# Conditional transformer block, eight groups in staggered beats: first norm begun four beats ahead of its old place, opening reordered, clears of va on VectorE, oT copied ahead of tanh

## Reference

```python
def _tc_rmsnorm(x, t, gw, gb, bw, bb):
    g = (t @ gw.T + gb)[:, None, :]
    b = (t @ bw.T + bb)[:, None, :]
    inv_rms = jax.lax.rsqrt(jnp.mean(x * x, axis=-1, keepdims=True) + EPS)
    return g * x * inv_rms + b

# attention: 16 heads of 8 features, softmax(q k^T / sqrt(8)) v, then Wo
# swiglu:    silu(x @ gate_w.T) * (x @ hid_w.T) @ out_w.T, 512 hidden features
y = x + _attention(_tc_rmsnorm(x, t, g1w, g1b, b1w, b1b), Wq, Wk, Wv, Wo)
y = y + _swiglu(_tc_rmsnorm(y, t, g2w, g2b, b2w, b2b), gate_w, hid_w, out_w)
out = x + y
```

## Time and profile before

| | us |
|---|---|
| median of 3 runs | 274.45 (273.54 to 274.57) |
| profiled execution | 273.25 |
| its span, first to last instruction | 271.2 |
| TensorE matmul busy | 228.1 (84%) |
| VectorE busy | 204.4 (75%) |
| ScalarE busy | 164.2 (61%) |
| GpSimd busy | 111.9 (41%) |

### The profile page before, as it was taken

How to read it: one execution, slowest core, us unless ns; L and a number is a source line. 1 busy time by engine, 2 the same in 40 slices (tenths; PEclk the granted TensorE clock), 3 DMA queues, 4 the chain that set the end, 5 groups by cost and what they waited for, 6 DMA issues and landing times.

```text
span 271.2 us, 8235 instructions
## 1 busy us (share of the span) xinstructions
PE 228.1 (84%) x3048; PEld 179.9 (66%) x3048; DVE 204.4 (75%) x489; ACT 164.2 (61%) x353; POOL 111.9 (41%) x183
## 2 busy tenths in 40 slices
PE   2436558977898999999999999999999899899895
PEld 2314236644666877787788778876887678677794
DVE  4655663497789798879887988888887888445573
ACT  5436373677586767775777677567656565565330
POOL 8244732173826272627262736252623232323320
PEclk9999755599999999999999999999999999999999
DMA  6758400260044004400350035003500000000001
GB/s 186 294 152 197 123 2 10 59 175 4 6 110 127 3 27 114 130 15 24 96 141 24 24 81 157 23 25 79 158 22 24 4 22 2 24 2 21 23 19 39
DMA packets 18818, 18.77 MB, mean 69 GB/s; under 512 B 3644, under 2 KB 17980, under 8 KB 18652
## 3 DMA queue, kind: packets, MB, share of 16 engines
q1 hardware_dynamic: 18252, 17.80, 23.4%
q10 hardware_dynamic: 528, 0.46, 0.7%
HBM read 3.22 MB, written 2.10 MB: 20 GB/s over the span
## 4 chain that ended last, share of the span: by engine, by line
PE 40%; issue 29%; POOL 14%; DVE 11%; ACT 5%; POOLq 0%; ACTq 0%
PE pv L423 5%; PE proj L483 5%; PE ffn L317 4%; PE score L406 3%; DVE nmax L748 3%; PE ffn L319 3%; PE ffn L318 3%; PE tok L442 2%; POOL inv L910 2%; POOL xn_lo L923 2%; PE raw L379 2%; PE proj L345 2%; POOL inv L881 2%; PE tok L438 2%; POOL xs L916 2%
## 5 line engine op out<-in xcount | busy, mean ns | idle before, releaser
L748 DVE TENSOR_REDUCE nmax<-raw 128x8 f32<-128x1024 f32 x61 | 74.2, 1217 | 6.7 <-PE raw L379 6.6
L591 ACT ACTIVATE p_s<-score 128x1024 f32<-128x1024 f32 x64 | 65.5, 1023 | 15.7 <-PE score L406 14.5
L423 PE MATMUL pv<-p_s,va 128*32 128x128 f32 x1024 | 42.8, 287 | 0.9 <-ACT xn L609 0.4
L620 ACT ACTIVATE th<-ffn 128x256 f32<-128x256 f32 x53 | 20.3, 384 | 27.7 <-PE ffn L319 27.4
L317 PE MATMUL ffn<-xn_hi,ffn_hi 128*128 128x256 f32 x106 | 34.7, 327 | 0.0
L483 PE MATMUL proj<-ffn_out_s,hT 128*128 128x128 f32 x256 | 33.8, 275 | 0.3 <-DVE x_s L816 0.3
L805 DVE SCALAR_TENSOR_TENSOR gated<-th,ffn 128x256 f32<-128x256 f32 x53 | 22.0, 415 | 15.8 <-ACT th L620 15.5
L483 PEld LDWEIGHTS proj<-ffn_out_s,hT 128*128 128x128 f32 x256 | 31.2, 191 | 0.6 <-issue 0.5
L423 PEld LDWEIGHTS pv<-p_s,va 128*32 128x32 f32 x1024 | 25.2, 112 | 8.5 <-issue 3.2
L319 PE MATMUL ffn<-xn_hi,ffn_lo 128*128 128x256 f32 x106 | 29.7, 280 | 0.0
L318 PE MATMUL ffn<-xn_lo,ffn_hi 128*128 128x256 f32 x106 | 29.6, 279 | 0.0
(11 more groups left out here) (123 smaller groups left out, 469.1 us busy)
## 6 DMA issues: line engine op xcount, KB each, us to landing
ks<-kp SPq DMA_DIRECT2D x48, 128.0 KB, 2.4
qs<-qp SPq DMA_DIRECT2D x45, 128.0 KB, 2.5
out_y<-x_s SPq DMA_DIRECT2D x16, 128.0 KB, 1.8
x_s<-in_x SPq DMA_DIRECT2D x1, 1536.0 KB, 9.6
qs<-shift SPq DMA_DIRECT2D x64, 4.0 KB
x_s<-in_x SPq DMA_DIRECT2D x2, 256.0 KB, 3.5
ffn_in_s<-in_ffn_in_w SPq DMA_DIRECT2D x1, 512.0 KB, 6.2
qs<-qp ACTq DMA_DIRECT2D x3, 128.0 KB, 3.6
```

Of the source, the lines that this page charges most:

```text
L423: mm = pe.matmul(pv[VW * j:VW * j + VW, (t % 2) * L:(t % 2 + 1) * L], va[vbuf(g)][:, t // 2, at:at + VW], p_s[:, (BEATS * g + t) % PBUF, p ...
L591: act.activation(p_s[:, n % PBUF, :], score[:], ACT.Exp, scale=SCALE).then_inc(s_exp, 1)
L748: dve.tensor_reduce(heads[:, :, t % 2, :], raw_dst(g, t)[:].rearrange("l (e j m) -> l e j m", e=HALVES, j=HQ), AX.X, ALU.max, negate=True) ...
```

## The change

MEAN moves from -24 to -28: squares, inverse root and scaling of a group are due four beats earlier, at T = 4, 12, 20 and 28 for groups 4 to 7; those of group 3, formerly in beat 0, go into the opening. In ScalarE's beat, the squares move from ahead of tanh to behind it, and the oT copy from behind tanh to ahead of it. In the opening, TensorE does the transposes of group 2 behind the fifth raw product and the transpose of maxima, alternating two banks; the two clears of va go from ScalarE to VectorE; VectorE does the high and low part of group 0 and the high parts of group 1 in another order; GpSimd sets the ones of the first va buffer ahead of the inverse root of group 2.

```diff
--- before.py
+++ after.py
@@ -61,7 +61,7 @@
     SCALE = float(DH) ** -0.5
     assert D == 128 and L == 128 and W == 512 and B % (2 * NB) == 0 and H * DH == D and HC == 4
 
-    MEAN, XT1, HI1 = -24, -23, -15
+    MEAN, XT1, HI1 = -28, -23, -15
     VALUE, KEY, QUERY = -7, -14, -13
     STACK = -12
     RAW, MAXT = -7, -3
@@ -219,7 +219,7 @@
         def xt1_dst(g, b):
             if g < 2:
                 return (score[:, 0:L], score[:, 512:512 + L], raw[:, 0:L], raw[:, 512:512 + L])[b]
-            return tok[:, 0:L] if early(g) else score[:, (b % 2) * 512:(b % 2) * 512 + L]
+            return (tok, ffn)[b % 2][:, 0:L] if early(g) else score[:, (b % 2) * 512:(b % 2) * 512 + L]
 
         def raw_dst(g, t):
             return score if g == 0 and t % 2 and t < BEATS - 1 else raw
@@ -326,7 +326,8 @@
                 elif g == 1:
                     pe.wait_ge(s_xn1, b + 1)
                 elif early(g):
-                    pe.wait_ge(s_xn1, NB * g + b)
+                    pe.wait_ge(s_xn1, NB * g + max(b - 1, 0))
+                    pe.wait_ge(s_qrest, 2)
                 pe.transpose(xt1_dst(g, b), xs1[:, g % 2, b, :], ident[:]).then_inc(s_xt1, 1)
 
             def a_values(g):
@@ -503,11 +504,11 @@
             b_raw(0, 1)
             a_values(0)
             b_raw(0, 2)
-            a_transpose(2, 0)
             b_raw(0, 3)
-            a_transpose(2, 1)
             b_raw(0, 4)
             b_maxT(0, 0)
+            a_transpose(2, 0)
+            a_transpose(2, 1)
             b_raw(0, 5)
             a_transpose(2, 2)
             b_raw(0, 6)
@@ -660,13 +661,10 @@
             a_middle(1, s_krest, k_rest, kp, s_kmid)
             a_middle(1, s_qrest, q_rest, qp, s_qmid)
             a_mean(2)
-            zero_fill(va[0][:].rearrange("l b v -> l (b v)"), s_va0[0])
-            a_norm(2, 0)
-            a_norm(2, 1)
             a_values(0)
-            a_norm(2, 2)
-            a_norm(2, 3)
-            zero_fill(va[1][:].rearrange("l b v -> l (b v)"), s_va0[1])
+            a_mean(3)
+            for b in range(NB):
+                a_norm(2, b)
             for T in range(LAST + 1):
                 for g, _ in due(T, KEY + 1, since=2):
                     a_high(g, s_k, key_dst(g), kp, s_khi)
@@ -678,12 +676,12 @@
                     c_ot(g, i)
                 for g, _ in due(T, KEY + 1, since=2):
                     a_middle(g, s_krest, k_rest, kp, s_kmid)
-                for g, _ in due(T, MEAN, since=3):
-                    a_mean(g)
+                for g, i in due(T, TRO, NB, 2):
+                    c_oT(g, i)
                 for g, p in due(T, FFN, PIECES):
                     d_tanh(g, p)
-                for g, i in due(T, TRO, NB, 2):
-                    c_oT(g, i)
+                for g, _ in due(T, MEAN, since=4):
+                    a_mean(g)
                 for g, i in due(T, XT2, NB, 2):
                     d_norm(g, i)
                 for g, b in due(T, XT1, NB, 2, since=3):
@@ -821,6 +819,10 @@
 
                 dve.memset(qs[u][:].bitcast(F32), 0.0).then_inc(s_zeroq[u], 1)
 
+            def zero_values(u):
+
+                dve.memset(va[u][:], 0.0).then_inc(s_va0[u], 1)
+
             dve.memset(ones[:], 1.0).then_inc(s_ones, 1)
             zero_queries(0)
             a_mean(0)
@@ -828,15 +830,18 @@
             a_mean(1)
             dve.wait_ge(s_attnw, 16)
             dve.tensor_copy(qk_hi[:], attn_w_s[:, 0:2, :]).then_inc(s_whi, 1)
+            a_hi(0, 0)
+            lo_first(0)
             scale_first(1)
-            for n in range(2):
-                a_hi(0, n)
-                lo_first(n)
+            a_hi(0, 1)
+            lo_first(1)
+            zero_values(0)
             a_rest(0, key_dst(0), kp, k_rest, s_khi, s_klo, s_krest)
-            a_rest(0, query_dst(0), qp, q_rest, s_qhi, s_qlo, s_qrest)
             a_hi(1, 0)
             a_hi(1, 1)
+            a_rest(0, query_dst(0), qp, q_rest, s_qhi, s_qlo, s_qrest)
             lowest_first(q_rest, qp, s_qmid, s_qlo)
+            zero_values(1)
             a_rest(1, key_dst(1), kp, k_rest, s_khi, s_klo, s_krest)
             a_rest(1, query_dst(1), qp, q_rest, s_qhi, s_qlo, s_qrest)
             for t in range(HQ):
@@ -965,9 +970,11 @@
             a_lo(1, 1)
             a_lowest(1, k_rest, kp, s_kmid, s_klo)
             a_lowest(1, q_rest, qp, s_qmid, s_qlo)
+            surround_values(0)
             a_inv(2)
             a_scale(2)
-            surround_values(0)
+            a_inv(3)
+            a_scale(3)
             zero_queries(2)
             zero_keys(2)
             surround_values(1)
```

## The result

The changed kernel takes 260.11 us (median of 4, 259.37 to 261.01) against 274.0 (273.07 to 274.57): ratio 0.950, 95% interval 0.9455 to 0.954.

A forecast was written before the change was run, and what follows sets the result against it. TensorE was taken as the bound from beat 8 on, with waits and a lower clock before. 12.8 us gained less 4.7 lost gave 8.1, so 266.3 us against the median of 274.45; range 261.5 to 271.0.

The forecast's parts named there:

- opening up to T2: Opening: reordered transposes, clears and casts start T0 near 32.65 and T2 near 39.9; 3.6 us gained, bounds 1.6 and 4.4.
- clock in beats 2 to 4: Early beats at TensorE's lower clock level: the sum counted no gain here; an earlier return was left to a rival.
- statistics out of T8: T8/T9: removing the mean ends TensorE's waits for a normalised tile and GpSimd's scaling; 1.58 us gained.
- statistics out of T16, T24, T32: Those beats: squares no longer hold back tanh, ending TensorE's 0.18 us wait for o_s each time; 0.54 us gained.
- oT ahead of tanh: Steady part: copying oT before tanh removes most of TensorE's 8.4 us in 17 waits; 7.1 us gained, bounds 3.5 and 8.4.
- statistics into T4: T4: oT copy, xs2 and the weights' lo part wait behind the moved block; 1.07 us lost, taken by likeness.
- into T12: T12: the moved block delays GpSimd's lo difference to 86.46, against 84.93; 1.53 us lost.
- into T20 and T28: T20 and T28: gate-and-up two beats on waits for the delayed lo difference; 1.07 us lost in T28, T20 alike.
- The clears: Opening: VectorE's two va clears, 1.82 us each, cost nothing; about 1 us for a GpSimd collision kept for the range.
- That rival: Opening and early beats: the clock returns earlier or never falls, worth 4.3 us, making 262.0; chance 0.18.
- The rival of a late clock: T4 and after: lower level lasts some 15 us longer, into T10 or T11; a microsecond more makes 277; chance 0.06.
- The worry that VectorE would take a part: Full beats: VectorE, 87% busy, takes half the oT gain, making 269.9; chance 0.16 together with the moved mean costing double.

The follow-up runs named there:

- e11: The changed kernel unaltered, measured again beside other runs on one chip: 260.63 us, ratio 0.958.
- e3: Changed kernel with MEAN = -24: statistics of groups 4 to 7 back in the group's first beat, ahead of oT and tanh; 260.52 us, ratio 0.959.
- e9: Changed kernel with GpSimd's inverse root and scaling one beat later and ScalarE's squares behind the normalisation: 257.92 us, ratio 0.945.
- e10: Kernel before with oT copy and tanh both ahead of the squares, which stay in the group's first beat: 264.50 us, ratio 0.973.
- e8: Changed kernel with only GpSimd's inverse root and scaling of groups 4 to 7 one beat later, behind the lo difference: 257.05 us, ratio 0.944.
- e4: Changed kernel with MEAN = -26, statistics in beats 6, 14, 22, 30: 259.81 us, ratio 0.952.
- e7: Changed kernel with MEAN = -26 and the squares behind the normalisation of the same beat: 257.75 us, ratio 0.947.
- e5: Kernel before with unread products added in TensorE's waits of the opening and beats 0 to 8: 278.23 us, ratio 1.021.
- e6: Changed kernel with the same kind of unread products added to keep TensorE busy early: 267.51 us, ratio 0.982.
- e1: Kernel before with one edit, ScalarE's oT copy ahead of tanh: 265.02 us, ratio 0.971.
- e2: Changed kernel with the oT copy back behind tanh: 269.70 us, ratio 0.990.

## Why the prediction was too small

The sum on record was 12.8 gained and 4.7 lost. Against the profiled pair:

| step | forecast | measured |
|---|---|---|
| opening up to T2 | -3.6 | -3.46, in it 0.9 lost to the clock |
| clock in beats 2 to 4 | 0 | -3.0 |
| clock at 54 to 58 us | 0 | +1.0 |
| statistics out of T8 | -1.6 | -1.46 |
| statistics out of T16, T24, T32 | -0.5 | -0.7 |
| oT ahead of tanh | -7.1 | -8.9 |
| statistics into T4 | +1.1 | +0.5 (beats 5 to 7: 8.72 in e11, 8.18 before) |
| into T12 | +1.5 | +1.61 |
| into T20 and T28 | +2.1 | +2.19 |

**The opening** came out near its number, T0 at 32.91 for 32.65 and T2 at 39.86 for 39.7, but partly by luck. The text had the shift release the score of T0. In both profiles the sixth maximum does, for which the code waits there: it ends at 32.77 (34.23 before), and the score follows at 32.91 (34.38). The times agree since the fifth maximum stands right behind the shift's split on VectorE. And the order is worth more than was forecast, 4.4 us: in e3 and e9, where the value products have the full level, T2 begins at 38.95 and 38.89. The changed kernel's profile lost 0.9 of it to the lower level at 24 to 26 us. In the old opening the same loss is hidden behind the wait for the scaling, for e10 has the slow value products too and begins T2 at 43.34. The six profiles with the new opening and slow value products, the first among them, have T2 between 39.62 and 40.01.

The clears show no cost, though no run has them alone. They took 1.82 us each, as estimated. The second ran from 18.09, beside the second of GpSimd's two lo differences:

```profile
17.11 1.86 POOL L900 TENSOR_TENSOR xn_lo<-xn,xn_hi 128x256 fp32r<-128x256 f32 x2
...
18.09 1.82 DVE L824 MEMSET va<- 128x2112 f32 x1 [0.39 <-issue]
```

In a window from 18.3 and in one from 39.7, the differences by themselves, first beside the clear, then with VectorE idle:

```profile
18.25 0.72 POOL L900 TENSOR_TENSOR xn_lo<-xn,xn_hi 128x256 fp32r<-128x256 f32 x1
```

```profile
39.60 0.73 POOL L900 TENSOR_TENSOR xn_lo<-xn,xn_hi 128x256 fp32r<-128x256 f32 x1
```

The first of the pair took 1.17 us; VectorE's difference of Q, which reads two inputs, ran beside it until 17.70. That the pair took 1.85 us in the kernel before says nothing of a clear, for there too it ran beside that difference.

By the sentence of the Trainium skill cited in the prediction (GPSIMD Engine Reference, Key points) a clear, which reads nothing, would not collide, and the trace agrees (0.72 us against 0.73).

**The statistics in T12, T20, T28** were right in size, and in T4 half as costly as taken by likeness. e8 shows GpSimd's block in front of the lo difference as the cause of the second beat's share, and e4, e7 and e9 that the first beat's share is ScalarE's order. The forecast had put both into one wait of 1.07 for the lo difference, and held that the wait for xn lies within it; they are two of 0.37 and 0.71 in different beats, and that their sum is 1.08 is luck.

**First step that failed: the clock.** The text read the lower level's stretch off one execution, took it for a property of the kernel, and gave its earlier return 0.18. e10 shows that beats 2 to 4 owe their 3.0 us to the level alone, e5 and e6 agree, and e1, e10 and e11 that the level varies between executions of one program. The profile on which the sum rested was one of the late ones, as by their spans (270.4 us or more in 16 of 27) most executions of the kernel before were. That rival's mechanism held; its price was 3.0 us by T5 and 2.5 by T8, and not 4.3. In the profiled pair 1.0 and 0.9 of the 3.0 are given back by the second stretch and the late first rise, so the clock makes 1.1 of the 12.1 us. Whether the denser opening causes the early return isn't settled. In all eight profiles with the new opening and no added products the level is back between 39.0 and 41.4 us, in the three with the old one at 44.5, 50.3 and 54.2, and the spread of the latter has no edit behind it.

The rival of a late clock held a wrong rate, though it did not come to be tested: 0.95 us a microsecond is what a full beat would lose per microsecond of its length at the full level. At the lower level such a beat takes up to twice as long, so a microsecond of that level costs at most half. The rise would have had to come later still than T10 or T11.

**Second step that failed: the size of oT.** The forecast added up the waits on TensorE's matmul rows, 8.4 us. The profile models the end of a matmul, and what is still running of it by that model covers part of the idle time. The weight load of the same product waited 12.4 us in 17 waits, 0.65 to 0.85 each from T11 on, and the beats shrank by that: 0.80 in beat 49, where the matmul row had 0.53. Take away the two in the first eight beats (1.0), T13 (0.7), and what remains in the five beats with the K copy (1.7, where the forecast had 0.5), and it makes 9.0, against the 8.9 of e2. The worry that VectorE would take a part was right for oT alone, where it took 2.0 of the 8.8 us from T10 on (e1 against e2), and void with the statistics moved: the text had the reason, that VectorE's run begins with the o_s that comes earlier, but did not see that this depends on tanh leaving its place behind the squares.

The range fell short at its low end because these two were independent and both on the same side. To the 8.1 of the forecast come 1.8 for oT, 1.1 for the clock, 0.8 for the opening's order and 0.5 for T4; that makes 12.3, against 12.1 in the spans, and the other rows are off by 0.2 at most. The medians, 13.9 apart, hold the rest, for the old median lies 0.75 above its profiled execution and the new one 0.9 below.

## What to carry to other kernels

Read what a stalled TensorE loses from the wait of the weight load, or from the length of the beat, and not from the matmul row alone. Before a sum rests on one execution, look at the granted clock of several: a stretch at the lower level that wanders from one to the next is a term of its own, with a price from the same beats at both levels. Ahead of the first change that the clock line records, read the level from the products' durations. And when work moves on a full in-order engine, follow it into every queue that it enters: here the squares, their block on GpSimd and the run on VectorE each had a price of their own, and the best version moved only GpSimd's part on by one beat.

## What was not expected of the hardware

Executions of one unchanged kernel on one core differ in when TensorE's clock falls and rises in the sparse opening, and their spans with it by some 3 us in 270: 268.6 or 268.7 us in two, 271.4 to 271.6 in five others on the same chip. One program, profiled three times up to T10, had the full level back at 44.5, 50.3 and 54.2 us, and T2 to T8 took 17.7, 20.3 and 20.3 us. The clock line can hide this: the profile with a mean granted clock of 1.0 ran its products at the lower level until 39.9 us. Products and waits added to keep the engine busy brought beats 2 to 8 to the full level and made the kernel before 6 us slower.
